# Two transformer layers on one core: loads, the first rotation and the filter's products put in another order

## The reference

```python
xn = layernorm(x)
x  = x + attention(xn, w_q, w_k, w_v)       # one head, rotary positions, causal softmax
       + moe_top1(xn, wg, W, b)             # 8 experts, capacity T / 8 = 512 tokens each
xn = layernorm(x)
h  = gelu(gelu(pos_emb @ W1 + b1) @ W2 + b2) @ W3 + b3   # the filter: 1024 x 128, no input in it
x  = x + (u * causal_fft_conv(v, h * decay)) @ Wo + bo   # u, v: projections of xn
       + moe_top2(xn)                       # 8 experts, the two best of each token
```

## Time and profile before

| | |
|---|---|
| median of 3 runs | 492.42 us (490.51 to 493.38) |
| the profiled execution | 493.04 us, span 491.2 us |
| mean granted TensorE clock | 0.934 of full speed |
| busy in the span | PE 366.0, VectorE 294.4, POOL 258.4, ScalarE 225.9 us |
| scatter of layer 0's rows by POOL | 32 indirect DMAs of some 1.08 us in the mean, 52.8 to 106.9 us |
| sends of layer 0's experts by POOL | 32 indirect DMAs, 117.5 to 165.7 us |
| DMA engines, tenths busy, slices of 12.3 us | 9 in the first eight slices, 2 or 3 after it |

### The profile page before, as it was taken

One profiled execution on the slowest core, in us unless ns is written; L12 is line 12 of the kernel. 1 busy time (PEld: TensorE's weight loads), 2 busy tenths in 40 slices (PEclk: granted clock), 3 DMA queues, 4 the chain that ended last, 5 costly groups with the idle time before them and its releaser, 6 DMA issues.

```text
span 491.2 us, 7805 instructions
## 1 busy us (share of the span) xinstructions
PE 366.0 (75%) x2302; PEld 298.7 (61%) x2302; DVE 294.4 (60%) x782; ACT 225.9 (46%) x551; POOL 258.4 (53%) x254
## 2 busy tenths in 40 slices
PE   2485588869997975949997978898887777766720
PEld 0272255658675644737996867787776667755620
DVE  3977569614773796474688993478438772244105
ACT  1373042325332316334343066434567676687724
POOL 2754766733666323016566676666666555365540
PEclk9999599997998999687998999999999999999975
DMA  9999999823321330001111282445322215422407
GB/s 211 396 197 262 166 140 135 268 51 85 87 75 40 111 89 1 1 5 39 34 34 37 69 261 75 142 140 151 112 69 75 63 29 158 137 74 74 126 11 252
DMA packets 64744, 55.05 MB, mean 112 GB/s; under 512 B 6819, under 2 KB 56683, under 8 KB 64446
## 3 DMA queue, kind: packets, MB, share of 16 engines
q1 hardware_dynamic: 57888, 41.71, 35.6%
q0 software_dynamic: 6656, 12.51, 8.4%
q10 hardware_dynamic: 158, 0.33, 0.4%
HBM read 30.44 MB, written 25.27 MB: 113 GB/s over the span
## 4 chain that ended last, share of the span: by engine, by line
PE 44%; issue 13%; ACT 12%; DVE 10%; DMA 10%; POOL 8%; SPq 1%; ACTq 0%; POOLq 0%; DVEq 0%
PE psS L1161 19%; PE psO L1161 15%; PE psT L1161 7%; ACT hT L1122 7%; POOL slots L826 4%; DMA slots<-row,slot 4%; DMA moe<-ys,xs 2%; POOL w L847 2%; DMA xres<-in_x 2%; ACT row L1027 1%; PE psT L1263 1%; POOL moe L836 1%; DVE work L1713 1%; DVE xres L1747 1%; DMA moe<-ys,ring 1%
## 5 line engine op out<-in xcount | busy, mean ns | idle before, releaser
L813 POOL DMA_INDIRECT slots<-row,slot x64 | 69.3, 1083 | 57.0 <-DVE slot L1580 22.4
L836 POOL DMA_INDIRECT moe<-ys,xs x61 | 61.1, 1001 | 58.3 <-issue 16.6
L1161 PE MATMUL psO<-ring,hT 128*128 128x128 f32 x320 | 45.2, 284 | 45.1 <-ACT hT L1122 45.1
L1161 PEld LDWEIGHTS psO<-ring,hT 128*128 128x128 f32 x320 | 38.7, 191 | 53.4 <-issue 53.4
L1122 ACT ACTIVATE hT<-psT,ring 128x128 f32<-128x128 f32 x160 | 45.6, 368 | 45.7 <-PE psT L1161 45.7
L1868 DVE TENSOR_TENSOR ys<-psO,ring 128x256 f32<-128x256 f32 x40 | 17.0, 424 | 75.3 <-PE psO L1161 75.1
L1055 ACT ACTIVATE ring<-w 128x642 f32 x80 | 55.9, 761 | 1.1 <-issue 1.0
L1161 PE MATMUL psS<-work 128*128 128x512 f32 (+3 forms) x96 | 42.6, 558 | 12.6 <-DVE work L1696 8.8
L836 POOL DMA_INDIRECT moe<-ys,w x35 | 38.0, 1087 | 23.3 <-DVE ys L1868 9.7
L1020 ACT ACTIVATE work<-psT 128x512 f32<-128x512 f32 (+3 forms) x32 | 16.5, 516 | 66.6 <-PE psT L1263 66.6
L826 POOL DMA_INDIRECT slots<-row,slot x32 | 34.9, 1091 | 18.1 <-DMA slots<-row,slot 10.9
(11 more groups left out here) (272 smaller groups left out, 781.4 us busy)
## 6 DMA issues: line engine op xcount, KB each, us to landing
slots<-xs SPq DMA_DIRECT2D x14, 516.0 KB, 14.7
mats<-in_iv SPq DMA_DIRECT2D x16, 256.0 KB, 3.7
xs<-slots SPq DMA_DIRECT2D x61, 64.5 KB, 1.9
w<-in_w SPq DMA_DIRECT2D x8, 321.0 KB
w<-slots SPq DMA_DIRECT2D x35, 64.5 KB, 1.9
xres<-in_x SPq DMA_DIRECT2D x4, 512.0 KB, 9.7
mats<-in_fw SPq DMA_DIRECT2D x1, 2048.0 KB, 11.3
moe<-xs SPq DMA_DIRECT2D x4, 512.0 KB, 7.8
```

Of the source, the lines that this page charges most:

```text
L813: pool.indirect_dma_start(slots1[:, :], bass.IndirectOffsetOnAxis(ap=(slot1, slot2)[k][:, i:i + 1], axis=0), row[:, i, :], None, bounds_ch ...
L836: pool.indirect_dma_start(dst[:, :], bass.IndirectOffsetOnAxis(ap=row_slots[l][m][:, D:ROWW].bitcast(I32), axis=0), ys[:, n % UNROLL, :], ...
L1161: return pe.matmul(o, lhsT, rhs, start=start, stop=stop)
```

## The change

- SP loads all of x (and the constants) before `wvg`; then `wqk` and `rope`; then the fill of `slots0`; the expert weights and biases; the fill of `moe0`; the 2 MB `mats`; and the fill of `slots1`. The weights of layer 1 are issued behind the first 16 row loads of layer 0 instead of during the scatter.
- The filter's first two layers leave the start and stand at rows 0 and 2 (PE, ScalarE) with the Tanh a row later. Both products of each activation become one VectorE instruction, (t + 1) * hx. Both layers use one PSUM bank pair, `S[0]`.
- The third layer goes to row 5, the radix passes to rows 6 to 8, the spectra to rows 9 and 10.
- PE projects batch 0's first half (`project(0, 0)`) between batch 1 and batch 2 of the gate logits, and `scores(0)` ahead of the counts; VectorE rotates it before the routing and takes the first row maximum in the middle of the routing.
- The experts of layer 0 begin at row 9 instead of 8, the splitting of the biases at row 12 instead of 9.

```diff
-FILT_RADIX_AT, FILT_DFT_AT = 3, 6
-SPLIT_AT = 9
+FILT_AT = (0, 2)
+FILT_RADIX_AT, FILT_DFT_AT = 6, 9
+SPLIT_AT = 12
-MOE0_FROM = 8
+MOE0_FROM = 9
...
@@ sync
                     sp.dma_start(cst[:, :], cst_in).then_inc(cst_loaded, 16)
-                    sp.dma_start(wvg, wvg_in).then_inc(w_a_loaded, 16)
-            sp.dma_start(mats[:, :, :, :], fw_in).then_inc(fw_loaded, 16)
+            sp.dma_start(wvg, wvg_in).then_inc(w_a_loaded, 16)
             sp.dma_start(wqk, wqk_in).then_inc(rope_loaded, 16)
             sp.dma_start(rope, rope_in).then_inc(rope_loaded, 16)
-            sp.dma_start(w0[:, :, :], w0_in).then_inc(moe0_w_loaded, 16)
...
             fill_slots(0, slots0, TILES0)
+            sp.dma_start(w0[:, :, :], w0_in).then_inc(moe0_w_loaded, 16)
...
+            sp.dma_start(mats[:, :, :, :], fw_in).then_inc(fw_loaded, 16)
             fill_slots(1, slots1, TILES1)
...
             for n in range(TILES0):
+                if n == UNROLL:
+                    sp.wait_ge(rad_f, RAD_F)
                 load_rows(0, slots0, n)
+                if n == RING[0] - 1:
+                    for a, b in [(w12[:, e, :], w12_in[e]) for e in range(E)] + [
+                            (wv[:, :], wv_in), (wu[:, :], wu_in), (wg1[:, :], wg1_in), (wo[:, :], wo_in)]:
+                        sp.dma_start(a, b).then_inc(l1_w_loaded, 16)
@@ gpsimd
-            inverse_std(0)
-            inverse_std(1)
-            filter_cubic(0)
-            inverse_std(2)
-            inverse_std(3)
-            filter_gelu(0)
-            filter_cubic(1)
-            filter_gelu(1)
+            for g in range(B):
+                inverse_std(g)
@@ scalar, in the loop over rows
+                if n in FILT_AT:
+                    act.wait_ge(filt_loaded, 32)
+                    filter_layer(FILT_AT.index(n))
+                if n - 1 in FILT_AT:
+                    filter_tanh(FILT_AT.index(n - 1))
@@ tensor
-            pe.wait_ge(filt_loaded, 32)
-            filter_layer(0)
             pe.wait_ge(cst_loaded, 16)
             pe.wait_ge(w_a_loaded, 16)
             for g in range(B):
                 transpose_tokens(g)
                 values_and_gates(g)
+                if g == 1:
+                    pe.wait_ge(rope_loaded, 32)
+                    project(0, 0)
...
-            filter_layer(1)
+            scores(0)
             pe.wait_ge(vg_free, 16)
             routing_counts(0, O[0])
...
                 if n + 1 < NT:
                     scores(n + 1)
+                if n in FILT_AT:
+                    filter_layer(FILT_AT.index(n))
@@ vector
+            def filter_cubic(k):
+                dve.wait_ge(f_act, 3 * k + 2)
+                stt(ht[0:FO, :], ht[0:FO, :], 1.0, hx[0:FO, :], ALU.add, ALU.mult).then_inc(f_dve, 1)
+
+            def filter_gelu(k):
+                dve.wait_ge(f_act, 3 * k + 3)
+                stt(hg[0:FO, :], hg[0:FO, :], 1.0, hx[0:FO, :], ALU.add, ALU.mult).then_inc(f_dve, 1)
...
             dve.wait_ge(rope_loaded, 32)
             rotate(0, 0)
+            dve.wait_ge(vg_free, 16)
+            dve.wait_ge(cst_loaded, 16)
+            first_layer_routing = routing0()
+            take(first_layer_routing, R0_OH)
+            row_max(0)
+            finish(first_layer_routing)
...
+                if n - 1 in FILT_AT:
+                    filter_cubic(FILT_AT.index(n - 1))
+                if n - 2 in FILT_AT:
+                    filter_gelu(FILT_AT.index(n - 2))
```

More of the change, by code:

```diff
@@ L458, in two_layer_kernel @@
         f_act = sem("f_act")
-        f_pool = sem("f_pool")
+        f_dve = sem("f_dve")
         filt_v_done = sem("filt_v_done")
@@ L601, in two_layer_kernel @@
                 S_USES.append(("s", n + 1))
+            if n in FILT_AT:
+                S_USES.append(("f", FILT_AT.index(n)))
         LAST_S, seen = {}, {}
         for use in S_USES:
-            slot = use[1] % 2 if use[0] == "s" else (use[1] + 1) % 2
+            slot = {"s": use[1] % 2, "pr": (use[1] + 1) % 2, "f": 0}[use[0]]
             LAST_S[use] = seen.get(slot)
@@ L705, in _ @@
             fill_slots(0, slots0, TILES0)
+            sp.dma_start(w0[:, :, :], w0_in).then_inc(moe0_w_loaded, 16)
+            sp.dma_start(y0.rearrange("p j d -> p (j d)"), b0_in.rearrange("e d -> (e d)").partition_broadcast(P)).then_inc(moe0_w_loaded, 16)
+            sp.dma_start(bias[:, :], bvuo_in.partition_broadcast(P)).then_inc(bias_loaded, 16)
             for i in range(0, NT, 8):
@@ L1196, in filter_layer @@
                 if k:
-                    pe.wait_ge(f_pool, 4 * k)
+                    pe.wait_ge(f_dve, 2 * k)
                 if k < 2:
+                    wait_scores_bank(("f", k))
                     for h in range(2):
                         r = (pe_sb[0:FO, :], hg[0:FO, :])[k][:, 512 * h:512 * h + 512]
-                        last = mm(S[k][0:FO, h, :], (f1w, f2w)[k], r)
+                        last = mm(S[0][0:FO, h, :], (f1w, f2w)[k], r)
                 else:
@@ L1254, in wait_scores_bank @@
                     kind, n = before
-                    pe.wait_ge(*((rope_mul, 2 * n + 2) if kind == "pr" else (exp_done, n + 1)))
+                    pe.wait_ge(*{"pr": (rope_mul, 2 * n + 2), "s": (exp_done, n + 1), "f": (f_act, 3 * n + 1)}[kind])
             def transpose_probs(n):
@@ L1314, in _ @@
                 values_and_gates(g)
+                if g == 1:
+                    pe.wait_ge(rope_loaded, 32)
+                    project(0, 0)
             pe.wait_ge(casts_done, 3)
             pe.wait_ge(ones_done, 2)
-            filter_layer(1)
+            scores(0)
             pe.wait_ge(vg_free, 16)
             routing_counts(0, O[0])
-            pe.wait_ge(rope_loaded, 32)
-            pe.wait_ge(f_act, 4)
-            project(0, 0)
-            pe.wait_ge(rt, R0_CUM)
-            scores(0)
+            pe.wait_ge(filt_loaded, 32)
             for n in range(NT):
@@ L1335, in _ @@
                         filter_spectrum(2 * (n - FILT_DFT_AT) + u)
+                if n == 1:
+                    pe.wait_ge(rt, R0_CUM)
                 if n:
@@ L1492, in norm_rows @@
                        ALU.mult).then_inc(xn_done, 1)
-            def norms(k0):
-                norm_stats(k0)
-                for k in range(k0 + 1, k0 + B):
-                    norm_stats(k)
-                    norm_rows(k - 1)
-                norm_rows(k0 + B - 1)
+            def filter_cubic(k):
[4 more added lines that the diff above has]
+                stt(hg[0:FO, :], hg[0:FO, :], 1.0, hx[0:FO, :], ALU.add, ALU.mult).then_inc(f_dve, 1)
             n_rt = [0]
@@ L1682, in _ @@
                 dve.memset(pickb[r:r + 1, :], 1.0).then_inc(pick_done, 1)
-            norms(0)
-            dve.wait_ge(vg_free, 16)
-            dve.wait_ge(cst_loaded, 16)
-            finish(routing0())
+            norm_stats(0)
+            norm_stats(1)
+            norm_rows(0)
+            norm_stats(2)
+            norm_rows(1)
+            norm_stats(3)
+            norm_rows(2)
+            norm_rows(3)
             def rotate(b, h):
```

28 lines of the change are left out of this document (2 added, 26 removed).

## The result

| | before | changed |
|---|---|---|
| median (range) of 20 runs each | 493.38 us (490.51 to 495.36) | 491.17 us (485.35 to 496.37) |
| the profiled execution | 493.04 us, span 491.2 | 495.55 us, span 493.7 |
| its mean granted TensorE clock | 0.934 | 0.914 |

By the ratio the change gains 0.75%, 3.7 us; by the medians of all twenty 2.2 us. I had forecast 7.0. The median lies 5.8 us above the forecast of 485.4, and 0.2 above my range of 481.5 to 491.0.

What follows compares the result with a forecast made beforehand. Bound: a chain of waits through POOL's filter products, 32 scatter DMAs and sends, then VectorE's adding. Terms -9.8 + 1.0 + 2.6 - 0.8 = -7.0 took 493.04 to 486.0, as a median 485.4 us; 8 in 10 range 481.5 to 491.

Steps and rivals of the forecast that it cites:

- Do the rows reach row 9 in time?: Rows 0 to 9 under the scatter: PE reaches the first expert's rows at 99.4 us, 2.3 before the data.
- rival 3: Filter layers in rows 0 to 3 fully serial, PE at 1.2 GHz: row 9 at 112, 495 us; chance 0.09.
- Start of the scatter, -9.8: Start, gate logits and routing: without POOL's filter products the scatter starts at 43.0 instead of 52.84 us.
- Length of the scatter, 55.0: POOL's 32 indirect DMAs, 54.0 us before: two of four new VectorE products hitting an issue add 1.0 us.
- Rival 2: Scatter stretched: each of four VectorE products blocks one issue whole, 6.8 instead of 1.0 us; 491.2 us; chance 0.08.
- Data to first send, +2.6: From first rows on chip to first send: 9.5 instead of 6.9 us, with spectra of 3.81 in between.
- Tail, -0.8: Sends to adding: the wait for rows goes, the wait for the result's load is next; 0.8 us gained.
- Rival 1: Rows late: radix right before the spectra brings PE to row 9 at 104 to 106; 488 to 490 us; chance 0.22.
- Rival 4: More gain: scatter loses slow pairs (3.3), logits 1 us earlier, rows ready ahead shorten adding; 481 to 482 us; chance 0.15.

Runs made afterwards that it cites:

- early trace: Profile of a further run of the unchanged changed kernel, granted clock 0.935: 483.89 us.
- late trace: Profile of the changed kernel's first profiled execution, granted clock 0.914: 495.55 us.

## Why the prediction was right and wrong

**What failed is the step "Do the rows reach row 9 in time?".** It said 99.4 us, 2.3 ahead of the data, "with a thin cover". The early trace has 100.55, close, and the late one 109.92, in both after the data. I priced PE's filter layer at 1.93 and the rest of the rows by the kernel before, whose clock is 1.00 from 62 to 108 us, so all at full clock; the late trace has the layer at 3.67 and a clock of 0.50 in three parts of that stretch, and 8.3 us of its delay are matmuls made longer by it. The move itself puts PE's waits of 3.6 and 1.4 us for the filter there. I had the half clock in the text, but as part of rival 3, with a chance of 0.09, and as something the rows' own work would prevent. The rival gave PE at 112 and a time of 495; the profiled execution has 109.92 and 495.55. Its other half, 7 us from a fully serial filter, isn't borne out: with the clock back, PE is at the rows at 100.55. The truth is between the forecast and that rival: nine of 20 executions take 492.5 to 496.4 us, the others 485.35 to 491.35. Shown: two courses of the same code that part by the clock (the two traces), and the clock held by added work (487.37, narrow). Not shown is what decides in one execution whether the clock holds: the late trace loses it at 81 and 105 us behind waits that the early one has as well. Nor is it shown why the eleven better executions, with a median of 490.0, stay above the forecast of 485.4; only the quickest execution of that kind has a trace.

A reading in that step is wrong without harm: the instruction at 65.39 is the scores of row 3 (512 columns; those of row 2, with 384, are at 64.14), and the scores of row 4 stand at 69.32. As far as I can redo the sum, its 61.5 and its 40.0 both count from the line at 65.39, so that 99.4 stands.

**Start of the scatter, -9.8.** Right: 43.0 forecast, 43.02 in the early trace and 44.07 in the late one. The single terms (normalising, the two inflated instructions, projection at 3.6) hold; the logits come at 34.0 and 35.0 where 34.6 was forecast.

**Length of the scatter, 55.0.** 54.65 from the first issue to the first reading back in the late trace, 52.8 in the early one. The difference is a pause of POOL before the 29th issue, 4.3 and 2.1 us, whose cause no trace names. The four products take 1.21 to 1.27 us, forecast 1.2. Rival 2 is wrong, and that its 491.2 is the measured median is luck: the issues beside the products take 0.97 to 1.49 us instead of 0.97. The Trainium skill (SBUF — State Buffer, "Who interferes with whom") says that a VectorE instruction with two SBUF inputs contends with a GpSimd instruction that reads SBUF, and calls the shared ports an exclusive lock. The Trainium skill also infers there that making a transfer's descriptors needs the write side of these ports, which such an instruction leaves free; the prediction left that out. The issues agree rather with this second part: in the early trace the one at 71.57 lies wholly inside a product (71.56 to 72.83) and takes 0.97, and none lost more than about 0.5 us beside a product of 1.2. Why some take longer stays open. Nor is the normalising (4.56 and 2.15 us), with one tile as input, a case of that sentence; one is the routing instruction of 2.07 us, which ended at 47.01, 0.3 us after POOL's pass of 44.39 to 46.72.

**Data to first send, +2.6.** The 9.5 us hold about: 8.9 from the expert's rows to the first send in both traces, with 3.74 of spectra in it. But what it counts from is PE's arrival and not the data, since PE never waits. So even the early trace owes its first send of 109.47 (forecast 111.2) to the rows, though by a microsecond only: its last rows are on chip at about 99.5.

**Tail, -0.8.** The mechanism is right, a wait for the load of the experts' rows before the adding, of 1.1 to 1.3 us. The sum isn't: 54.4 to 54.5 from first send to adding instead of 53.5, because the load of the result is issued 50.3 us after the first send, 49.5 before.

**Rival 1** (rows late by the radix passes) isn't borne out: in both traces PE's last two waits ahead of the spectra are of 1.1 us each, and with the clock back PE is at the rows at 100.55.

**Rival 4** (481 to 482) needed rows ready ahead. No execution of the changed kernel has them; the versions with the filter back in the start do, at 484.06 and, with the late rotation, 482.03.

**The balance.** In the early trace the adding is at 163.87 (forecast 164.8) and the time 483.89. In the late one it is at 173.36, 1.6 later than before, and the time 495.55: the 9.4 us lost in the rows eat all of the 8.8 gained at the scatter's start. The median of 491.17 lies between.

## What to carry to other kernels

When a stage that hid other work is shortened, its cover is a quantity to compute at both clock levels: here a step moved under it brought waits for PE, the low clock came behind the waits, and every matmul of the stretch paid for it. Look at the spread and the clock of many executions, not at one: the range that grew from 5 to 11 us here came from a clock that sometimes held and sometimes didn't. Take the part of a change that frees an engine (products on VectorE) without the part that only moves work into a stretch that becomes critical (layers into rows 0 to 2).

## What the runs showed of the hardware

- One program on one core has courses 12 us apart (483.89 and 495.55 us), with the same waits of PE up to the expert's rows; up to there the granted clock was 0.50 in 38 to 48 and 58 to 65 us in one, and in 37 to 50, 57 to 70, 81 to 88 and 105 to 108 in the other.
- 21 matmuls without use took the median from 491.17 to 487.37 us and the range from 11 to 2.4 us.
- After a wait of 9.26 us for data the spectra, which take 3.74 us at full clock, took 4.31, with a granted clock of 0.50 from 96 to 106 us.
- Beside VectorE products of 1.2 us with two inputs in SBUF, POOL's issues of indirect transfers took 0.97 to 1.49 us; the median of all is 0.97.
